# A four-layer transformer block: who prepares the last stage's tiles, where pooled products and turned tiles stand in the coattention, and where attention's value products stand among its scores

## What is computed

```
x = x + tanh(g_xattn[0]) * attention(layernorm(x), ctx)      # 16 heads of 16, 512 keys a batch, rope, softmax
x = x + tanh(g_ffn[0])   * experts(layernorm(x))             # 8 experts, top 2, and a shared one
x = x + tanh(g_xattn[1]) * coattention(layernorm(x), ctx)
x = x + tanh(g_ffn[1])   * bitffn(layernorm(x))
```

```
coattention(e, c):  Sim = e@w1 + c@w2 + (e*w3)@c.T + b;  A = softmax(Sim);  h = A@c
                    pool = softmax(rowmax(Sim)) @ e                  # one vector a batch
                    out  = [e, h, e*h, e*pool] @ W_qv + b_qv
bitffn(x):          bit(x, w) = quant(x, 127/max|x| by row) @ ternary(w)
                    out = bit(silu(bit(x, w_gate)) * bit(x, w_up), w_down)    # 256 -> 1024 -> 256
```

## Time and profile before

| what | us |
|---|---|
| median of 3 runs | 730.57 |
| the profiled execution's own time | 729.56 |
| its span in the trace | 727.3 |
| attention, from the first row maximum to the last copy | 63.8 to 261.3 |
| coattention | 498 to 646.7 |
| last stage | 647.0 to 727.3 |

### The profile page before, as it was taken

How to read it: one execution, slowest core, us unless ns; L and a number is a source line. 1 busy time by engine, 2 the same in 40 slices (tenths; PEclk the granted TensorE clock), 3 DMA queues, 4 the chain that set the end, 5 groups by cost and what they waited for, 6 DMA issues and landing times. The chain is left out here.

```text
span 727.3 us, 9826 instructions
## 1 busy us (share of the span) xinstructions
PE 658.4 (91%) x3348; PEld 414.3 (57%) x3348; DVE 458.0 (63%) x778; ACT 340.6 (47%) x598; POOL 311.2 (43%) x482
## 2 busy tenths in 40 slices
PE   4997899999999878989999999997899999986885
PEld 2663434343434247656777878774668576853553
DVE  4877888888888237497343433435374655469894
ACT  2554588888888863544222223422311212013564
POOL 9757657586444407500010100101131717256796
PEclk9997599999999999999999999998989999988999
DMA  8469945636300058003000000001000000000001
GB/s 270 149 240 268 199 44 85 90 52 88 47 1 1 1 194 327 16 0 125 5 1 1 0 0 0 1 0 59 1 0 1 0 1 0 1 0 9 30 29 50
DMA packets 23143, 43.40 MB, mean 60 GB/s; under 512 B 4060, under 2 KB 10848, under 8 KB 22336
## 3 DMA queue, kind: packets, MB, share of 16 engines
q1 hardware_dynamic: 15224, 31.02, 12.7%
q0 software_dynamic: 6048, 10.03, 10.3%
q10 hardware_dynamic: 1832, 1.84, 1.2%
HBM read 32.27 MB, written 10.49 MB: 59 GB/s over the span
## 5 line engine op out<-in xcount | busy, mean ns | idle before, releaser
L722 DVE TENSOR_REDUCE mx<-ps_f 128x2 f32<-128x1024 f32 x128 | 151.4, 1220 | 27.5 <-PE ps_f L660 27.2
L825 ACT ACTIVATE prob<-ps_s 128x512 f32<-128x512 f32 x256 | 134.6, 608 | 34.2 <-PE ps_s L678 34.1
L678 PE MATMUL ps_s<-q_stacks,k_stacks 53*128 53x512 f32 x256 | 90.1, 484 | 5.7 <-ACT prob L825 3.3
L678 PEld LDWEIGHTS ps_s<-q_stacks,k_stacks 53*128 53x128 f32 x256 | 35.8, 188 | 86.9 <-ACT prob L825 70.8
L660 PE MATMUL ps_f<-k_stacks,q_stacks 53*128 53x512 f32 x256 | 64.4, 454 | 6.8 <-DVE mx L722 4.7
L687 PE MATMUL ps_o<-prob,vst 128*32 128x512 f32 x512 | 69.0, 612 | 0.0
L1310 DVE SCALAR_TENSOR_TENSOR h<-ps_u,most,qs 128x512 f32<-128x512 f32 x32 | 24.0, 750 | 62.7 <-ACT qs L1240 62.7
L180 POOL TENSOR_TENSOR norm_tmp_att<-st 128x4 f32<-128x4 f32 x4 | 1.0, 240 | 145.4 <-DVE st L1349 145.4
L1240 ACT ACTIVATE qs<-ps_g 128x512 f32<-128x512 f32 x40 | 23.9, 597 | 82.5 <-PE ps_u L1111 82.5
L749 POOL TENSOR_TENSOR q_stacks<-minus,q_stacks 128x1024 fp32r<-128x1024 f32 x16 | 38.0, 2373 | 37.8 <-ACT minus L816 35.9
L1817 ACT ACTIVATE qs<-ps_SC,nmax 128x512 f32<-128x512 f32 x16 | 11.0, 688 | 68.0 <-DVE nmax L1703 68.0
(11 more groups left out here) (305 smaller groups left out, 1478.4 us busy)
## 6 DMA issues: line engine op xcount, KB each, us to landing
k_stacks<-room_k POOLq DMA_DIRECT2D x18, 256.0 KB, 5.7
q_stacks<-room_q POOLq DMA_DIRECT2D x18, 256.0 KB, 5.3
up<-in_up SPq DMA_DIRECT2D x10, 256.0 KB, 6.4
x<-in_x SPq DMA_DIRECT2D x4, 512.0 KB, 10.6
ctx_raw<-in_ctxTC SPq DMA_DIRECT2D x4, 512.0 KB, 6.6
room_k<-k_high SPq DMA_DIRECT2D x4, 512.0 KB, 4.6
room_k<-k_low SPq DMA_DIRECT2D x4, 512.0 KB, 6.4
room_q<-q_high SPq DMA_DIRECT2D x4, 512.0 KB, 5.8
```

The lines of the kernel that those rows point to most:

```text
L678: pe.matmul(ps_s[n % 3][:, :], ks[rows(h), 2 * s + pair, kt * P:(kt + 1) * P], qs[rows(h), 2 * s + pair, :], start=True, stop=True).then_i ...
L722: dve.tensor_reduce(mx[:, f % 2, qt, 2 * pair:2 * pair + 2], ps_f[n % 2][:, :, :], AX_X, ALU.max).then_inc(used, 1)
L825: act.activation(prob[:, kt % 2, j, :], ps_s[n % 3][:, :], ACT.Exp, scale=SCALE)\
```

## The change

- Attention: PE's order within a step is written out; `values` of tiles 3 (of the step before), 0, 1 and 2 stand behind score (0,3), behind score (1,2), behind score (3,0) and behind score (3,3), and first scores stand partly in pairs.
- Coattention: `pooled` stands behind the third output tile, with `pooled_weights` and the normalisation of the next batch on DVE moved up too; `wx` has two buffers; the transposes of the next batch come in two halves, one before the fourth output tile and one at the batch's end (behind a wait for `out_used`); five idle products end PE's program; `batch_scales(1)` comes in between the last batch's tiles.
- Last stage: DVE scales tiles from tile 2 on (`scaled`), POOL only rounds them, and in POOL's order `rounded(n - 1)` stands ahead of `quantise(n + 2)`; ACT copies the turned tiles (`x_transposed`), makes `ys` (`down_scale`) and normalises the last batch (`normalise`, by a `shift` that POOL computes); `batch_scales(2)` comes ahead of the first `hidden`.

```
...
+                scores(s, 2, 0)
+                scores(s, 2, 1)
+                if s + 1 < STEPS:
+                    maxima(s + 1)
+                scores(s, 2, 2)
+                ahead(s, 5)
+                scores(s, 2, 3)
+                scores(s, 3, 0)
+                values(s, 1)
+                scores(s, 3, 1)
+                ahead(s, 6)
+                ahead(s, 7)
+                scores(s, 3, 2)
+                scores(s, 3, 3)
...
-    if n % QT == 0:
-        pool.wait_ge(early["scales_ready"], n // QT + 1)
-    pool.tensor_scalar(early["xr"][:, u, :], xn[:, n, :], early["amax"][:, SX, n:n + 1], MAGIC, ALU.mult, ALU.add)\
-        .then_inc(early["xr_done"], 1)
+    if turned is None:
+        pool.wait_ge(early["scales_ready"], 1)
+        scaled_tile(pool, early, xn, n, u)
     pool.wait_ge(early["xr_done"], n + 1)
     if turned is not None:
         pool.wait_ge(turned, n - 1)
...
-                transposes(b, v)
...
                 feature(2)
+                pooled(b, v)
                 context(b, 3)
                 context_transposes(b, 2)
+                if not last:
+                    transposes(b + 1, 1 - v, 0)
                 feature(3)
-                pooled(b, v)
                 context_transposes(b, 3)
+                if not last:
+                    if before:
+                        pe.wait_ge(out_used, b * QT)
+                    transposes(b + 1, 1 - v, 1)
...
+            for i in range(2):
+                transposes(0, 0, i)
             batches(pe, batch, weight_sums)
             for q in range(QT):
                 features(B - 1, (B - 1) % 2, q)
+            idle_products(pe, ps_S[0][:, 0:P], id32, 5)
...
-                transposed(b, v)
+                transposed(b, v, 1)
+                similar_rows(b, v)
...
                 updated(2)
+                if not last:
+                    normalise(b + 1, 1 - v)
+                pooled_weights(b, v)
                 context(b, 3)
                 context_transposed(b, v, 2)
+                if not last:
+                    transposed(b + 1, 1 - v, 0)
                 updated(3)
-                if not last:
-                    normalise(b + 1, 1 - v)
-                pooled_weights(b)
                 context_transposed(b, v, 3)
...
-            for q in range(QT):
+            residual(B - 1, 0)
+            batch_scales(dve, early, ffn, xn, wstat, 1)
+            for q in range(1, QT):
                 residual(B - 1, q)
...
             for n in range(T + 3):
+                if live(n - 1):
+                    rounded(n - 1, 1 - n % 2)
                 if live(n + 2):
                     quantise(pool, early, xn, n + 2, n % 2, xT_done)
                 if n == 0:
                     batch_statistics(pool, per, ffn, B - 1)
-                if live(n - 1):
-                    rounded(n - 1, 1 - n % 2)
+                    pool.tensor_tensor(shift[:, :], ffn["tmp"][:, 4, (B - 1) * QT:], ffn["tmp"][:, 8, (B - 1) * QT:],
+                                       ALU.mult).then_inc(shift_ready, 1)
                 if live(n - 3):
                     residual(n - 3, 1 - n % 2)
...
-                dve.tensor_scalar(ys[:, ds(n, 1)], hs[:, u, 1:2], gd[:, 0:1], None, ALU.mult).then_inc(ys_ready, 1)
...
             def step(n, u):
-                if live(n + 1):
-                    transposed(n + 1, 1 - u)
+                if live(n + 2):
+                    scaled(n + 2, u)
+                if isinstance(n, int) and n == 0:
+                    batch_scales(dve, early, ffn, xn, wstat, 2)
+                    dve.wait_ge(early["scales_ready"], 3)
                 if live(n):
                     hidden(n, u)
-                if isinstance(n, int) and n == 0:
-                    batch_scales(dve, early, ffn, xn, wstat, 2)
-                if isinstance(n, int) and n == 1:
-                    normalise_late(dve, per, ffn, B - 1, ffn["normed"])
                 if isinstance(n, int) and n == 3:
                     batch_scales(dve, early, ffn, xn, wstat, B - 1)
-            transposed(0, 0)
-            batch_scales(dve, early, ffn, xn, wstat, 1)
+                    dve.wait_ge(early["scales_ready"], B)
+
+            def scaled(n, u):
+                dve.wait_ge(xq_ready, n - 1)
+                dve.tensor_scalar(xr[:, u, :], xn[:, ds(n, 1), :].rearrange("p o d -> p (o d)"), amax[:, SX, ds(n, 1)],
+                                  MAGIC, ALU.mult, ALU.add).then_inc(early["xr_done"], 1)
+            dve.wait_ge(early["scales_ready"], 2)
             schedule(dve, step)
...
+            def x_transposed(n, u):
+                act.wait_ge(xT_done, n + 1)
+                wait(act, up_done, n - 1)
+                act.copy(xqT[:, u, :, :], ps_x[:, :, :]).then_inc(xT_ready, 1)
+
+            def down_scale(n, u):
+                act.wait_ge(f_ready, n + 1)
+                act.activation(ys[:, ds(n, 1)], hs[:, u, 1:2], ACT.Copy, scale=gd[:, 0:1]).then_inc(ys_ready, 1)
+
+            def normalise():
+                act.wait_ge(shift_ready, 1)
+                for q in range(QT):
+                    t = (B - 1) * QT + q
+                    last = act.activation(xn[:, t, :], x_sb[:, t, :], ACT.Identity, scale=ffn["tmp"][:, 8, t:t + 1],
+                                          bias=shift[:, q:q + 1])
+                last.then_inc(ffn["normed"], 1)
...
             def step(n, u):
+                if live(n + 1):
+                    x_transposed(n + 1, 1 - u)
                 if live(n):
                     silu(n, u)
+                if live(n - 1):
+                    down_scale(n - 1, 1 - u)
                 if live(n - 3):
                     scaled(n - 3, 1 - u)
                 if live(n - 2):
                     transposed(n - 2, u)
+                if isinstance(n, int) and n == 1:
+                    normalise()
+            x_transposed(0, 0)
             schedule(act, step)
```

80 lines of the change are left out of this document (44 added, 36 removed).

## The result

The changed kernel took 725.85 us (median of 6 runs, 723.01 to 728.11), the kernel before 729.81 beside it: a ratio of 0.9933, 95% interval 0.9907 to 0.9959. That is 4.0 us less by the medians and 4.9 by the ratio, where 12.7 were forecast. The profiled execution took 727.60, its span is 725.7.

The account below looks back on a forecast made before the run. Bounds: in attention engines taking turns, in coattention PE with boundary waits and lowered clock, in the last stage DVE and POOL. Terms -4.6 - 9.3 - 4.5 + 5.2 = -13.2, with 0.5 for slow clock -12.7: 717.9 us, range 708.5 to 726.

Parts of the forecast that it names:

- a chain closes over two tiles: ... 8.6 for two tiles, 4.3 a tile: Last stage, tiles 4 to 15: POOL's rounding behind both passes closes a chain; 46.1 against 40.85, +5.2 us.
- In every second tile ... I count this wait; the 4.3 has room for it.: Last stage: DVE's scaling waits for POOL's pass in every second tile, within the 4.3 a tile.
- rival 2: Last stage: DVE's scaling waits for POOL's pass in every tile, 4.57 instead of 4.3 a tile; 724, chance 0.12.
- 19 instead of 23.2: Last stage, tile 0 to 4: scales and normalisation leave DVE's path, tile 2 waits; -4.2 of a -4.5 us term.
- Net 0.3 a step, 15 steps: -4.6 us.: Attention: values of tile 0 behind three scores save 0.52, values of the last step cost 0.2; bounds 0 and 7.8.
- At the two later boundaries ... 2 x 2.2: Coattention: wait of 1.52 becomes 0.8, and the slow-clock stretch of 1.52 goes, at each of two boundaries; 4.4 saved.
- coattention -9.3: Coattention in all: 4.4 at later boundaries, 2.0 from batch 0 to 1, 2.9 in the last batch; lower bound 2.5.
- Moved work costs the same where it stands; what counts are the waits: Coattention: premise of the -9.3 us, that only removed or added waits change the time.
- 1 (POOL's rounding in time): Last stage: rounding is not the bound, DVE's pace rules, 40.8 in place of 46.1; 710, chance 0.17.
- 3 (the clock falls throughout the last stage): Last stage: PE's idle time lowers the clock, 1.7 more a pair, 8.5 for five; 726, chance 0.08.
- 4 (attention gains nothing): Attention: pairs of first scores wait for DVE by 0.3 a step, so no gain; 722.5, chance 0.12.
- 5: Attention: DVE lags a maximum at both pairs, 2.3 a step lost over 15 steps, kernel slower; 752, chance 0.04.

Follow-up runs that it names:

- e_order: Changed kernel with POOL's rounding of tile n+2 again ahead of the two passes of tile n-1: 713.14 us, ratio 0.9767 to the kernel before.
- pe_order: Changed kernel with PE doing gate and up before the next tile's transposes, ACT silu before the copy: 714.61 us, ratio 0.9826.
- after_xr: Changed kernel with tile scaling given back to POOL, behind the two passes: 730.56 us, ratio 1.0003.
- o_pool: e_order with POOL's quantising of the three coattention weights moved behind its all-reduce in batches 1 and 2: 716.41 us, ratio 0.9838.
- before_look: The kernel before, unchanged, profiled once more: 726.62 us (a single execution).
- o_oldatt: e_order with attention wholly as before the change: 714.64 us, ratio 0.9808.
- e_att2: Kernel before with only attention's new order of values, a second run of that version: 727.23 us, ratio 0.9964.
- att_end: e_att2's kernel with the last two of attention's 16 steps in the old order: 727.09 us, ratio 0.9949.
- o_idle2: e_order plus idle PE products in attention's last step and a half and at the next stage's start: 713.80 us, ratio 0.9782.

## Why the prediction was wrong in size

The sign and most mechanisms held; three terms came out worse than forecast. Two were right in mechanism and wrong in size or incomplete (the chain of the last stage, the waits of the coattention); in attention a step was missing, what the new order does to the granted clock. By the parts run alone, the miss of 7.8 us (12.7 less 4.9) is about 3.5 in the last stage, 2.8 in attention and 1.3 in the coattention, each with an interval of 2 us or more to either side.

- **"a chain closes over two tiles: ... 8.6 for two tiles, 4.3 a tile", +5.2 us.** The mechanism was right, shown from both of its links (e_order, pe_order) and by lengthening it (after_xr). Its size was not: 9.0 in three of the five pairs (8.97 in the one shown). Of the 0.37 too much, 0.15 is POOL's first pass, 1.35 instead of 1.20: DVE's scaling starts 0.07 before it (687.36 and 687.43), and the pass took 1.27 instead of 1.12. Another 0.14 lies between silu and the product and 0.08 at the rounding. These three pairs make 1.2 of the 2.6 us that the stretch missed by. The other 1.4 is one pair of 9.98, with the lower clock from 680.7 to 684.1; for the clock the whole stage had been allowed 0.5. The fifth pair took 8.62, as forecast. Together 48.66 instead of 46.1. The whole stage alone cost 4.7 by its ratio, against +0.7 and 0.5 of clock forecast; its profile shows 3.6 of it (-3.7 and +7.3).
- **"In every second tile ... I count this wait; the 4.3 has room for it."** Right: the scaling at 691.60 took 0.96 instead of 0.35 beside POOL's pass and ended 0.25 before silu did (691.70 + 1.11). So rival 2 (a wait in every tile) did not come. What the prediction left out is that the wait goes both ways: the pass behind DVE's scaling is the longer. The section of the Trainium skill it cited (SBUF — State Buffer, SBUF: two separate sides), by which whoever starts first holds the ports, fits both rows in direction: the first is not lengthened (the pass of 1.12 at 691.29, the scaling of 0.35 at 687.36), the second is. Its other page (Perfetto Trace Analysis, Optimizing Scalar/DVE Operations), by which moving work between the two might not help, did not decide: with either order on POOL the first four tiles are 1.7 shorter with DVE scaling (19.00 and 20.65, 16.05 and 17.76).
- **"19 instead of 23.2"** for tile 0 to 4: measured 19.00, with tile 2 late as worked out (5.19 behind tile 1).
- **"Net 0.3 a step, 15 steps: -4.6 us."** Most steps were 10.89 (forecast 10.86), but two of the 15 took 11.42 in every profile with the new order, which loses 1.1. So with the clock alike, attention and the stretch behind it together take 240.6 with the new order (pe_order, o_pool) and 243.8 with the old (before_look, o_oldatt): 3.2 less instead of 4.6. The step that failed is the one that was not there: what the new order does to the granted clock.

  Of the ten profiles with the new order throughout and without idle products, eight have a stretch of the lower level between 242 and 272, 6.8 to 20.5 us long; with the old order none of five has. If both orders were equally prone to it, that would come about by chance in under 1 of 100 cases (an estimate by counting). Where the stretch is 6.8 long, the same two pieces take 242.3 to 242.7, and where it is 17.1 long, 245.2 in e_att2 and 246.7 to 247.0 in three others, whose lower level at attention's start was longer too. The mean of the ten is 244.2, the same as that of the five with the old order: in the profiles the clock takes back the whole gain. The timed runs do not say it as sharply, -0.9 and -2.6 us with intervals that reach from +1.3 to -4.9. What in the order brings the fall stays open: it is there with the last two steps in the old order (att_end), it is missing in pe_order and o_pool, and idle products removed it and gained nothing measurable (o_idle2).
- **"At the two later boundaries ... 2 x 2.2", coattention -9.3.** At the boundaries it was right to 0.1 (waits of 0.82, tiles at the higher level). It failed in mid-batch: "Moved work costs the same where it stands; what counts are the waits" overlooked that POOL's quantising and all-reduce did not move along. From the second batch's first similarity to the third's, 1.7 came off, and from the third's to the fourth's 0.2: two waits there (0.85 where it was 0.23, and 1.35) give back 1.97 of the 2.2. The last batch gained 1.0 instead of 2.9: it has two longer waits in mid-batch too (0.74, for ACT, where it was 0.23, and 0.36) and one of 0.68 for DVE, since the added scales did not fit between its tiles. That makes 1.55 of the 1.9. From batch 0 to 1, 4.1 came off where 2.0 was counted; that batch end was at the lower level before (528.1 to 534.9) and is not now, which is the likely reason for the rest.
- **Rivals.** 1 (POOL's rounding in time) is ruled out for this kernel and true of e_order, whose 713.1 lies near its 710. 3 (the clock falls throughout the last stage) did not come; one stretch of 3.4 from tile 4 on cost 1.4. 4 (attention gains nothing) is the nearest in result, by another mechanism than the one named: DVE's maxima were in time. 5 did not come. The range's upper end, 726.0, was just enough; the forecast of 717.9 lay 8 too low. The 0.90 for a gain of over 0.5% came true with 0.67%, by little: for a sum of terms of both signs, each with bounds several us wide, it was too sure.

## What to carry to other kernels

When an in-order program moves one engine's step behind another, walk the chain through all engines until it closes and divide by the tiles it spans: two lines of order on the least busy engine were worth 12.7 us here, more than all that the change took off the busy time of DVE (0.8) and POOL (5.1). When a boundary wait is removed, look for work of an off-path engine that keeps its own time: the batch that starts sooner meets it in the middle. And where PE is idle in many short pieces, a new order's gain in steady state is not yet its gain in time; compare the granted clock over several runs.
